# Split input of the down product in every second layer-0 tile

## The reference

```python
coef = jnp.zeros((T, E), topk_w.dtype).at[jnp.arange(T)[:, None], topk_idx].add(topk_w)
g = jnp.einsum('th,ehi->tei', x, Wg)
u = jnp.einsum('th,ehi->tei', x, Wu)
h = jax.nn.silu(g) * u * coef[:, :, None]
moe_out = jnp.einsum('tei,eih->th', h, Wd)
shared = jax.nn.silu(x @ SWg) * (x @ SWu) @ SWd
return (moe_out + shared).reshape(orig_shape)
```

## Time and profile before

| | |
|---|---|
| median of three runs | 1779.66 us (1776.04 to 1780.97) |
| span of the profiled execution | 1724.1 us |
| PE busy | 1679.7 us, 97% |
| DVE busy | 1350.6 us, 78% |
| ACT busy | 812.6 us, 47% |
| POOL busy | 609.5 us, 35% |
| mean granted TensorE clock | 0.989 of full speed |

### The profile page before, as it was taken

The page is one execution under the profiler, slowest core; times in us unless marked ns, Lnnn a source line. Parts: engine busy times, 40 slices in busy tenths (PEclk is TensorE's granted clock), DMA queues, the critical chain, the costliest instruction groups (busy, mean ns, idle before and its releaser), DMA issues.

```text
span 1724.1 us, 24432 instructions
## 1 busy us (share of the span) xinstructions
PE 1679.7 (97%) x7020; PEld 1188.6 (69%) x7020; DVE 1350.6 (78%) x3866; ACT 812.6 (47%) x1456; POOL 609.5 (35%) x656
## 2 busy tenths in 40 slices
PE   5999999999999999999999999999999999999995
PEld 4667777777777777777777777777777766667773
DVE  5878888888888787979797979787888776565558
ACT  4535453636363545454544445454545343554431
POOL 3311242424242324233333232332323233567770
PEclk8999999999999999999999999999999999999998
DMA  8949474646373747373737373645546445577758
GB/s 211 201 104 256 100 187 105 178 109 181 99 181 101 182 103 194 97 200 86 202 84 192 85 189 90 174 106 135 144 106 167 99 109 154 191 266 266 237 173 312
DMA packets 172339, 273.89 MB, mean 159 GB/s; under 512 B 14312, under 2 KB 57320, under 8 KB 171952
## 3 DMA queue, kind: packets, MB, share of 16 engines
q1 hardware_dynamic: 163632, 254.63, 56.1%
q0 software_dynamic: 8576, 17.70, 3.2%
HBM read 202.15 MB, written 65.93 MB: 155 GB/s over the span
## 4 chain that ended last, share of the span: by engine, by line
PE 94%; DVE 2%; ACT 1%; issue 1%; DMA 1%; POOL 0%; SPq 0%; POOLq 0%; DVEq 0%; ACTq 0%
PE ps_y L709 26%; PE ps_gate L660 8%; PE ps_gate L661 8%; PE ps_gate L662 8%; PE ps_up L662 8%; PE ps_up L660 8%; PE ps_up L661 8%; PE ps_y L735 4%; PE ps_side L675 3%; PE ps_side L758 1%; PE ps_side L852 1%; PE ps_side L835 1%; PE ps_side L794 1%; PE ps_side L819 1%; PE ps_side L660 1%; PE ps_side L661 1%
## 5 line engine op out<-in xcount | busy, mean ns | idle before, releaser
L918 DVE TENSOR_TENSOR silu_h<-ps_up,silu_h 128x512 f32<-128x512 f32 x618 | 424.0, 686 | 295.3 <-ACT silu_h L1325 243.3
L1325 ACT ACTIVATE silu_h<-ps_gate 128x512 f32<-128x512 f32 x618 | 367.6, 598 | 567.4 <-PE ps_gate L662 565.1
L709 PE MATMUL ps_y<-silu_h,w_dn 128*128 128x512 f32 x1056 | 542.7, 595 | 3.0 <-DVE silu_h L912 3.0
L912 DVE TENSOR_TENSOR silu_h<-coef_b,silu_h 128x512 f32<-128x512 f32 x528 | 386.8, 732 | 13.0 <-DMA coef_b<-coef_kept 9.2
L660 PE MATMUL ps_gate<-xnT,w_gu 128*128 128x512 f32 x528 | 342.7, 649 | 0.0
L709 PEld LDWEIGHTS ps_y<-silu_h,w_dn 128*128 128x128 f32 x1056 | 199.7, 189 | 53.7 <-issue 7.7
L660 PE MATMUL ps_up<-xnT,w_gu 128*128 128x512 f32 x528 | 207.9, 394 | 4.6 <-DVE silu_h L918 4.6
L661 PE MATMUL ps_gate<-xnT,w_gu 128*128 128x512 f32 x528 | 209.4, 397 | 0.0
L662 PE MATMUL ps_gate<-xnT,w_gu 128*128 128x512 f32 x528 | 208.9, 396 | 0.0
L662 PE MATMUL ps_up<-xnT,w_gu 128*128 128x512 f32 x528 | 208.0, 394 | 0.0
L661 PE MATMUL ps_up<-xnT,w_gu 128*128 128x512 f32 x528 | 206.8, 392 | 0.0
(11 more groups left out here) (267 smaller groups left out, 2454.8 us busy)
## 6 DMA issues: line engine op xcount, KB each, us to landing
coef_b<-coef_kept SPq DMA_DIRECT2D x254, 512.0 KB, 6.8
slots_x<-empty SPq DMA_DIRECT2D x15, 2080.0 KB, 12.7
w_block<-w_kept SPq DMA_DIRECT2D x45, 512.0 KB, 3.9
xs<-slots_x SPq DMA_DIRECT2D x37, 260.0 KB, 3.8
y_back<-y_kept SPq DMA_DIRECT2D x15, 512.0 KB, 7.0
w_down<-in_ffn_w SPq DMA_DIRECT2D x45, 128.0 KB, 3.7
w_raw<-in_ffn_w SPq DMA_DIRECT2D x33, 128.0 KB, 7.9
xres<-in_x SPq DMA_DIRECT2D x16, 256.0 KB, 3.1
```

What stands on the lines that cost most here:

```text
L709: eng.matmul(ps_y[:, :], w_dn[:, j], silu_h[:, g % HBUFS], start=j == 0, stop=last).then_inc(pe_down)
L912: eng.tensor_tensor(silu_h[:, s], coef_b[:, q % COEF_RING, k], silu_h[:, s], ALU.mult).then_inc(dve_h)
L918: eng.tensor_tensor(silu_h[:, s], ps_up[g % 2][:, :], silu_h[:, s], ALU.mult).then_inc(dve_h1)
L1325: eng.activation(silu_h[:, s], ps_gate[g % 2][:, :], ACT.Silu).then_inc(act_silu)
```

## The change

In tiles with odd j (16 in each chunk, 256 in all):

- GpSimd multiplies silu by the coefficients (`silu_coef`), at the head of its step g. VectorE's `times_up` then waits for that in place of ScalarE, and its result is the whole h.
- ScalarE rounds h into `h_hi` (`h_round`, at the head of step g + 2, before silu).
- VectorE subtracts the rounded part from h, into `h_lo` (`h_rest`, at the head of step g + 2). `times_coef` is left out.
- TensorE makes the down product of three rounded products, as the gate and up products are made. The down weights of odd tiles are therefore split too: they join the gate and up weights in `w_raw` and in `w_two`, and ScalarE's and GpSimd's splits of those tiles cover 384 columns where they covered 256.

Even tiles stay as they are. Beside that: `w_dn` holds the even tiles alone; the loads for layer 1 wait for `pe_down` with other counts; in chunk 15 the scatters of chunk 13 are planned in tiles 10 to 17 (ROUTE1_THEN); and the scratch in SBUF for the descriptors of GpSimd's DMAs is set to 2048 bytes.

```diff
-TILES_UNDER_XS, TILES_UNDER_XST, TILES_UNDER_WEIGHTS = 9, 15, 27
+TILES_UNDER_XS, TILES_UNDER_XST, TILES_UNDER_WEIGHTS = 8, 12, 22
 HBUFS = 4
+HI_BUFS, LO_BUFS, SPLIT_LATE = 2, 1, 2
...
+ROUTE1_THEN = [(at, what) for at, what in ROUTE1 if not what.startswith("send")] + [(43 + n, f"send{n}") for n in range(TOP1 * ROWS)]
...
-        plan[g] += [(what, c - 2) for at, what in ROUTE1 if at == j + TILES0 and c > 1]
+        plan[g] += [(what, c - 2) for at, what in (ROUTE1 if c < SPARSE else ROUTE1_THEN) if at == j + TILES0 and c > 1]
...
+                if odd(g):
+                    n, w = odd_before(g), weights0(j)[:, 2]
+                    hi, lo = h_hi[:, n % HI_BUFS], h_lo[:, n % LO_BUFS]
+                    eng.wait_ge(act_hhi, n + 1)
+                    eng.matmul(ps_y[:, :], w[:, 0], hi, start=False, stop=False)
+                    eng.matmul(ps_y[:, :], w[:, 1], hi, start=False, stop=False)
+                    eng.wait_ge(dve_h, scaled_before(g) + 1)
+                    eng.matmul(ps_y[:, :], w[:, 0], lo, start=False, stop=False).then_inc(pe_down)
+                    return
...
+            def h_rest(g):
+                n = odd_before(g)
+                eng.wait_ge(act_hhi, n + 1)
+                if n >= LO_BUFS:
+                    eng.wait_ge(pe_down, odd_at(n - LO_BUFS) + 1)
+                eng.tensor_tensor(h_lo[:, n % LO_BUFS], silu_h[:, g % HBUFS], f32(h_hi[:, n % HI_BUFS]), ALU.subtract).then_inc(dve_h)
 
             def times_up(g):
                 s = g % HBUFS
-                eng.wait_ge(act_silu, g + 1)
+                if odd(g):
+                    eng.wait_ge(pool_coef, odd_before(g) + 1)
+                else:
+                    eng.wait_ge(act_silu, g + 1)
...
             for g in range(STEPS):
-                if g >= 1:
+                if odd(g - SPLIT_LATE):
+                    h_rest(g - SPLIT_LATE)
+                if g >= 1 and not odd(g - 1):
                     times_coef(g - 1)
...
+            def h_round(g):
+                n = odd_before(g)
+                eng.wait_ge(dve_h1, g + 1)
+                if n >= HI_BUFS:
+                    eng.wait_ge(pe_down, odd_at(n - HI_BUFS) + 1)
+                eng.copy(h_hi[:, n % HI_BUFS], silu_h[:, g % HBUFS]).then_inc(act_hhi)
...
+                if odd(g - SPLIT_LATE):
+                    h_round(g - SPLIT_LATE)
                 if TILES_FIRST <= g < TILES + UNITS1:
                     silu(g)
...
+            def silu_coef(g):
+                s = g % HBUFS
+                q, k = wait_coef(eng, g)
+                eng.wait_ge(act_silu, g + 1)
+                eng.tensor_tensor(silu_h[:, s], coef_b[:, q % COEF_RING, k], silu_h[:, s], ALU.mult).then_inc(pool_coef)
...
             for g in range(STEPS):
+                if odd(g):
+                    silu_coef(g)
                 for what, key in plan[g]:
                     step(what, key, g)
...
-    nc = bacc.Bacc("TRN2", target_bir_lowering=False, num_devices=1)
+    nc = bacc.Bacc("TRN2", target_bir_lowering=False, num_devices=1, dynamic_dma_scratch_size=2048)
```

74 lines of the change are left out of this document (49 added, 25 removed).

## The result

| | before | changed |
|---|---|---|
| median of the runs, us | 1778.49 (1776.04 to 1780.97) | 2007.9 (1999.98 to 2011.22) |
| ratio, 95% interval | 1 | 1.129 (1.127 to 1.132) |
| profiled execution, span, us | 1724.1 | 2004.8 |
| layer 0, from the trace, us | 1456.0 | 1686.3 |

A forecast was written before the change was run, and what follows sets the result against it. TensorE, busy for 97% of the span, was taken as the bound. Eight chunks at 9.9 us, five at 8.1, plus 5.5, 4 and 4, saving included, made 133 us more: 1910 us, range 1855 to 1965.

The forecast's parts named there:

- The saving: Odd-tile down products on TensorE: three split products replace one plain fp32 product, 0.20 us less in 256 tiles, 51 us.
- rival D: Split products with the new operands cost more than 0.23 us each, adding 0 to 50 us; chance 0.02.
- Step (1): Tiles 5 to 9: VectorE's multiplication reading tile 7's up product ends at 759.2, stalling tile 9's up product 0.8 us.
- Steps (2) and (3): Tiles 9 to 13, GpSimd's queue: 2.9 us stall, TensorE 2.6 us later; tiles 11 to 15, late silu: about 6.1.
- Step (4): Tiles 15 to 23: GpSimd's queue adds 2.4 us with the weight split, 0.6 without; exponentials at tile 19 add 1.9.
- Step (5): Tiles 24 to 32 and 0 to 4 have slack: -0.8 us saving, +0.3 for tile 29's product behind message additions.
- VectorE keeps its count: Odd tiles: the subtraction h_rest replaces the multiplication by coefficients on VectorE, same shape, 0.68 us in such rows.
- The size of a collision: VectorE and GpSimd holding each other up: priced at 0 to 0.7 us, taken only where they meet on the path.
- the wide reading: Any GpSimd instruction reading SBUF blocks VectorE's two-input ones: up to 1.3 us more a chunk, 21 us in 16.
- Rival C: Stalls of 3 us bring TensorE's clock down to 1.2 GHz: 1965 to 2010 us; chance 0.04.
- Rivals A and B: First: engines have slack, gain arrives, 1728 to 1750 us, chance 0.13; second: gain just eaten, 1785 to 1840, chance 0.11.
- The signs: TensorE's share about 90%, waits on silu_h, chunk 8 at 97 to 100 us, tile 11's multiplication waiting 3 to 5.

The follow-up runs named there:

- no_rest: no_product also without VectorE's subtraction h_rest; the third of the three down products reads the rounded part again: 1729.34 us, 0.975 of before.
- memset_waited: Changed kernel with three GpSimd memsets replacing its product, VectorE's multiplication still waiting for them, one buffer for the rounded part: 1932.01 us, 1.088 of before.
- no_product: Changed kernel without GpSimd's product by coefficients in odd tiles; VectorE's multiplication waits for silu as before, rounding and subtraction stay: 1791.08 us, 1.008 of before.

## Why the prediction was right or wrong

**The saving: right.** 0.20 us in 256 tiles, 51 us. no_rest shows 1729.3 for a sum of 1728, and 86.5 us a chunk where it was 89.37: 2.85 us of the 3.2, with the rounding in it. That also answers rival D.

**Step (1): MUL(7) right, the stall not.** I had MUL(7) end at 759.2 on the clock of the kernel before. It ended at 876.74 in the changed kernel, whose chunk began 117.45 later: 759.29. But UP(9) was 1.65 us late, not 0.05. The term that the step lacks is TensorE's transpose at tile 8. It waits for a bank that VectorE frees right after MUL(7):

```profile
876.88 0.17 DVE L1183 TENSOR_TENSOR left<-ps_side,left 128x8 f32<-128x8 f32 x1
```

```profile
877.10 0.66 PE L800 MATMUL ps_side<-common,rows 128*128 128x128 f32 x4 [2.05 <-DVE left L1183]
```

I had listed who queues behind a waiting MUL on VectorE, and not who waits for those for a bank.

**Steps (2) and (3): right in mechanism and nearly in size.** MUL(11) was to end at 773.0; it ended at 891.25, which is 773.80. MUL(13) was to end at 781.6 and ended at 782.6. UP(13) was 3.42 us late for a forecast 2.6, UP(15) 7.05 for 6.1; the start of it is step (1). GpSimd's queue between q_turned and the product is as added up (compare; the columns are those of the timeline):

```profile
884.02 1.28 POOL L1596 TENSOR_TENSOR qf<-qf,q_turned 128x512 f32<-128x512 f32 x1 [2.15 <-DVE q_turned L1102]
...
887.76 1.53 POOL L1599 TENSOR_SCALAR tmp<-qf 128x512 f32<-128x512 f32 x1
889.24 1.29 POOL L1662 TENSOR_TENSOR silu_h<-coef_b,silu_h 128x512 f32<-128x512 f32 x1
```

**Step (4): right, 0.8 us short.** From UP(15) to UP(21) the loss grew by 5.1 us for a forecast 4.3.

**Step (5) failed.** "-0.8 for the saving and +0.3" gave -0.5; from UP(21) to the next chunk it was +5.2 in chunk 8 and +3.6 in chunk 12 and most others. It nearly holds where collisions are absent (memset_waited, -0.1 from UP(21) on). I had written that I take the collision "only where the two meet below", and then looked for meetings in tiles 5 to 13 alone. In tiles 24 to 32 VectorE was 92% busy, so the 1.1 us that a coefficient product loses there has nowhere to go. Over chunks 2 to 9 the forecast was short by 51 us (845.6 against 8 x 99.3), over 10 to 14 by 27, and in chunk 8 5.7 of the 7.5 us arise behind UP(21).

**"VectorE keeps its count" failed as a reason for nothing.** The count is the same, and yet no_product, with TensorE's 51 us saved, is 14 us slower than the kernel before, with no GpSimd product in the picture. That is 65 us lost, and 62 of them go with the rest. It heads VectorE's queue and waits there for ScalarE, and MUL of an odd tile comes third in a row where it came second.

**The size of a collision.** I priced it at 0 to 0.7 us from one row (1.38 for 0.68). Measured means over all 272 coefficient products are 957 ns against 715 in memset_waited, and single ones lose 1.09 (1.77) and, in the worst meeting, 2.55 (3.23). The Trainium skill, SBUF — State Buffer, "Who interferes with whom", says that a VectorE instruction with two SBUF inputs contends with a GpSimd one that reads SBUF, but not with one that only writes it, and that who is issued first decides. The runs agree on the first two: 150 us with reads, none to speak of with memsets. On the third the rows are divided. Where both operations read two tensors, the later one is the one held up, as at 338.07 and 338.14 above, but the coefficient product at 887.50 started ahead of the minimum and was held up, and the one at 767.73 in the kernel before started 0.77 us behind it and was not. I had set the wide reading aside on that one meeting; its 21 us would still have been far short of the 76.

**Chunks 0, 1, 15**: +11.5, +8.6 and +12.4 for forecasts 4, 5.5 and 4, 19 us of the 97. I did not take them apart.

**Rival C** was priced as no addition on the path, and the measured time lies in its range, by luck. In chunk 8 TensorE dropped to its lower level, 1.2 of 2.4 GHz, for parts of tiles 15, 19 and 31, each time behind stalls; a window of 4 us around tile 31 (columns as above) has a granted clock of 0.63:

```profile
950.00:954.00 4.00, 3.33 (x7) 1.99 (x8) 3.90 (x19) 1.12 (x2) 3.00 (x4) 0.63 0.32 65
```

TensorE was busy for 1756 us in the changed kernel and 1646 in no_rest, with the same 7276 instructions, so 110 us of its busy time are matmuls at the lower level or stretched by waits. In the steady chunks the lower level costs nothing that can be seen. Chunks 4 and 7 are of the same kind:

```profile
427.90:533.03 105.13, 95.34 (x393) 67.78 (x392) 80.54 (x224) 52.51 (x96) 50.18 (x46) 0.95 0.48 122
744.99:850.12 105.13, 91.31 (x394) 65.18 (x392) 80.53 (x224) 52.47 (x96) 50.24 (x46) 1.00 0.49 122
```

Chunk 4 spent about 10 us at the lower level (a granted clock of 0.95 is a tenth of the time at half speed), chunk 7 none, and both took 105.13 us. Chunks 0 and 15 and layer 1 have no such pair. **Rivals A and B** were both refuted by MUL(11) and MUL(13) being as late as worked out, or later.

**The signs.** Of those that I had named, TensorE's share (88%), its waits for VectorE's silu_h and VectorE's for GpSimd's came as written. Chunk 8 took 106.7 us and not 97 to 100, and MUL(11) itself stood idle for GpSimd only 1.61 us and not 3 to 5; the rest of its lateness came with the work in front of it.

## What to carry to other kernels

Before an elementwise operation moves from VectorE to GpSimd, count on VectorE every operation with both inputs in SBUF, over the whole loop and not only at its tight place, and let each meet a GpSimd read once; where VectorE was 92% busy here, that time was lost. Compare with a memset of the same length in the operation's place, once waited for and once not: the two runs separate the wait from the collision, to within the 8 us by which a memset shifts other work. And an operation on the way to an engine that may only run two tiles ahead is the wrong one to move: the same engine pair with the subtraction, which nothing waited for until three tiles later, cost 150 us less.

## What the hardware showed

- A GpSimd product of 128x512 with two SBUF inputs beside VectorE's: 1.26 us alone, up to 1.84 beside it, and VectorE's 0.68 became 1.77, and 3.23 where a GpSimd minimum stood in front of the product. With nobody waiting, 256 of them cost 150 us, on 1791.
- GpSimd memsets of the same length cost nothing in the sum (0.2 us). A one-input GpSimd operation cost 40 us; VectorE behind it took 1.10 us when it started 0.06 us after it and 0.69 from 0.66 us on.
- MUL, with one input in PSUM, kept its 681 to 688 ns on average in every kernel.
- Chunks with 10 us and with no time at TensorE's lower level took the same 105.13 us, with other engines on the path.
- One execution of a kernel had a layer 1 of 268 us at 223 to 233 GB/s, all others 311 to 321 us; a span from one profile is no base for a sum across stages.
